# A graph network on one Trainium2 core: every other turn's eighth source tile picked column by column by ScalarE instead of gathered

## The reference

```python
hs = h[src]
m = sum_b coef[etype, b] * (hs @ bases[b])        # layers 0-2; layers 4, 5: (x @ W[etype])[src]
h_new = relu(segment_sum(m, dst, n) + h @ loopw + bias)
```

## Time and profile before

| | |
|---|---|
| Median of 3 runs | 7757.05 us (7752.96 to 7761.15) |
| The profiled execution | 7750.85 us, of which the span from the first to the last instruction is 7749.0 us |
| GpSimd busy | 5606.2 us (72%) |
| TensorE (PE) busy | 5240.5 us (68%) |
| VectorE (DVE) busy | 3236.1 us (42%) |
| ScalarE (ACT) busy | 1009.2 us (13%) |
| TensorE's granted clock, mean | 0.682 of full speed |
| Indirect gathers in relational layers | 3276 + 819 |

### The profile page before, as it was taken

How to read it: one execution, slowest core, us unless ns; L and a number is a source line. 1 busy time by engine, 2 the same in 40 slices (tenths; PEclk the granted TensorE clock), 3 DMA queues, 4 the chain that set the end, 5 groups by cost and what they waited for, 6 DMA issues and landing times. The chain is left out here.

```text
span 7749.0 us, 133241 instructions
## 1 busy us (share of the span) xinstructions
PE 5240.5 (68%) x25966; PEld 4651.5 (60%) x25967; DVE 3236.1 (42%) x10580; ACT 1009.2 (13%) x2622; POOL 5606.2 (72%) x6200
## 2 busy tenths in 40 slices
PE   6777777777776666667777777667776766544444
PEld 5667666766656555667666766556655655533333
DVE  5454454554555555544444662222223333212222
ACT  1111111111111111122222011111111111100000
POOL 6777767777767777677777337777767777677776
PEclk7777777677777777655555887777677777655555
DMA  3222222222222222222222652222222222212222
GB/s 107 79 78 76 78 75 74 78 78 78 78 55 56 57 58 57 60 66 65 66 65 66 181 148 55 57 59 57 59 54 56 58 57 59 54 53 57 55 56 54
DMA packets 348777, 538.27 MB, mean 69 GB/s; under 512 B 124457, under 2 KB 204823, under 8 KB 347975
## 3 DMA queue, kind: packets, MB, share of 16 engines
q0 software_dynamic: 184416, 378.91, 18.2%
q1 hardware_dynamic: 115315, 127.96, 5.9%
q10 hardware_dynamic: 48500, 26.51, 1.2%
HBM read 448.48 MB, written 80.14 MB: 68 GB/s over the span
## 5 line engine op out<-in xcount | busy, mean ns | idle before, releaser
L680 POOL DMA_INDIRECT ring<-h_table,edges_i x3276 | 3136.8, 958 | 1075.6 <-issue 1032.9
L968 PE MATMUL sum<-onehot,ring 128*128 128x128 f32 x8320 | 1737.9, 346 | 1014.7 <-DMA ring<-h_table,edges_i 802.0
L968 PEld LDWEIGHTS sum<-onehot,ring 128*128 128x128 f32 x8320 | 1399.2, 240 | 1313.5 <-DMA ring<-h_table,edges_i 778.5
L1267 DVE TENSOR_TENSOR acc<-msg,acc 128x16 f32 x4160 | 727.7, 175 | 2682.4 <-PE msg L975 2167.2
L975 PE MATMUL msg<-work,mix_w 128*128 128x128 f32 x4992 | 1032.3, 391 | 278.6 <-ACT work L760 271.7
L975 PEld LDWEIGHTS msg<-work,mix_w 128*128 128x128 f32 x4992 | 954.3, 294 | 352.5 <-issue 332.6
L760 ACT ACTIVATE work<-sum 128x512 f32<-128x512 f32 x1040 | 619.9, 597 | 3719.2 <-PE sum L968 3631.6
L629 POOL DMA_INDIRECT sorted_rows<-ring,pos_i x832 | 805.8, 969 | 283.0 <-issue 245.8
L680 POOL DMA_INDIRECT ring<-in_x_dram,edges_i x819 | 798.8, 975 | 280.8 <-issue 253.9
L661 POOL DMA_INDIRECT ring<-h_table,pos_i x832 | 786.7, 945 | 275.3 <-issue 275.3
L975 PE MATMUL msg<-work,rel_w 128*128 128x128 f32 x3328 | 731.8, 409 | 182.8 <-ACT work L760 181.0
(11 more groups left out here) (197 smaller groups left out, 3628.1 us busy)
## 6 DMA issues: line engine op xcount, KB each, us to landing
lent<-h_table SPq DMA_DIRECT2D x6656, 0.5 KB
ring<-sorted_rows SPq DMA_DIRECT2D x208, 260.0 KB, 3.1
ring<-h_table,edges_i POOLq DMA_INDIRECT x3276
edges_i<-bucket_flat SPq DMA_DIRECT2D x208, 208.0 KB
lent<-in_x_dram SPq DMA_DIRECT2D x1664, 0.5 KB
h_table<-rows ACTq DMA_DIRECT2D x78, 256.0 KB
ring<-h_table SPq DMA_DIRECT2D x832, 8.0 KB
sorted_rows<-ring,pos_i POOLq DMA_INDIRECT x832
```

The lines of the kernel that those rows point to most:

```text
L680: nc.gpsimd.indirect_dma_start(out=rows_in[:, s, :], out_offset=None, in_=rows_of[:, :], in_offset=bass.IndirectOffsetOnAxis(ap=srcT_i[:, ...
L968: last = nc.tensor.matmul(SUM[q % 2][:, t * KEYS:(t + 1) * KEYS], rows_in[:, 4 * q + t, :], onehot[:, 4 * q + t, :], start=True, stop=True)
L1267: nc.vector.tensor_tensor(acc[:, at], MSG[h][:, s * WIN:(s + 1) * WIN], acc[:, at], ALU.add).then_inc(added, 1)
```

## The change

In layers 0, 2, 4 and 5 (not 1) GpSimd skips tile 7 (`PICKED`) in turns 2, 4, ..., 50. In place of each skipped gather ScalarE copies the 128 source columns of the transposed table into `picks` [128 x 128], 64 in a turn, so that a tile is filled over two turns. It does 16 after each quarter's evacuation: it loads 16 source numbers into registers and issues 16 ACTIVATEs of 128x1, each with a source and a destination column that lie in registers. At the end of every turn TensorE waits for the 64 picks, transposes `picks` into `SUM[1]`, and ScalarE copies the result into slot 7 or, after a turn with only half of a tile, into a part of the ring that nothing reads. TensorE waits for that copy (`picks_placed`) before quarter 1 of the next turn. The source numbers of the next turn come by a DMA of 64 numbers, issued by ScalarE at the end of a turn. In layer 1 ScalarE only raises the four semaphores.

```diff
+PICKED = HALF - 1
+PICKS = D // 2
 # GpSimd
+                                if s == PICKED and picks_in_layer(l) and i and i % 2 == 0:
+                                    continue
 # ScalarE
+                    def list_picks(i):
+                        at = nc.s_assert_within(act.snap(i // 2 * (2 * RING * D - D) + i * PICKS + (2 * RING + PICKED) * D),
...
+                        act.dma_start(picks_i[:, :], src[bass.ds(at, PICKS)].rearrange("(o e) -> o e", o=1)).then_inc(picks_in, 16)
+                    def pick(i, k, q):
+                        each = PICKS // 4
+                        if q == 0:
+                            act.wait_ge(picks_in, k * 16 + 16)
+                            apart(act)
+                            act.wait_ge(picks_turned, k + 1)
+                            apart(act)
...
+                        _, sources = nc.values_load_multi_w_load_instructions(
+                            picks_i[0:1, q * each:(q + 1) * each], engines=[ACTIVATION], min_val=0, max_val=N_NODES - 1,
...
+                        for e in range(each):
+                            last = act.activation(picks[:, bass.ds(first + (q * each + e), 1)],
+                                                  nodes[layer["src"]][:, bass.ds(sources[e], 1)], ACT.Copy)
+                        if q == 3:
+                            last.then_inc(picks_set, 1)
+                    def place(i, k):
+                        list_picks(nc.s_assert_within(act.snap(i + 1 - (i + 13) // 64 * TURNS), min_val=0, max_val=TURNS - 1,
...
+                        act.wait_ge(picks_turned, k + 2)
+                        act.wait_ge(summed[1], k + 2)
...
+                        act.activation(ring[:, bass.ds(to, D)], SUM[1][:, 0:D], ACT.Copy).then_inc(picks_placed, 1)
 # ScalarE's evacuate, behind each quarter's copy and at the end of the turn
+                                if picks_in_layer(l):
+                                    pick(i, k, q)
+                        if picks_in_layer(l):
+                            place(i, k)
 # TensorE's messages
+                                if q == 1:
+                                    pe.wait_ge(picks_placed, k + 1)
...
+                        if picks_in_layer(l):
+                            pe.wait_ge(picks_set, k + 1)
+                            nc.tensor.transpose(SUM[1][:, 0:D], picks[:, :], ident[:, :]).then_inc(picks_turned, 1)
```

More of the change, by code:

```diff
@@ L34 @@
 SP = mybir.EngineType.SP
+ACTIVATION = mybir.EngineType.Activation
 D = 128
@@ L424, in build, with picks_in_layer, gathers, gathers_before @@
         rows_from = [x] + [tables[(l - 1) % 2] for l in range(1, len(LAYERS))]
-        def gathers(s):
+        def picks_in_layer(l):
+            return l != 1
+        def gathers(s, l):
+            if s == PICKED and picks_in_layer(l):
+                return 16 * (TURNS // 2 + 1)
             return GATHER_PASS - 16 * QUADS if s == RING - 1 else GATHER_PASS
+        def gathers_before(s, l):
+            return sum(gathers(s, n) for n in range(l) if LAYERS[n]["kind"] == REL)
         def apart(eng):
@@ L606, in _ @@
             nc.gpsimd.memset(group_end[:, 0:1], 0).then_inc(lanes_set, 1)
+            nc.gpsimd.memset(picks[:, :], 0.0).then_inc(lanes_set, 1)
             pool.wait_ge(src_in, 16)
@@ L685, in _ @@
                         pool.wait_ge(summed[3], count(P, p, r, TURNS) + 1)
+                        pool.wait_ge(picks_placed, count(P, p, r, TURNS) + 1)
                         apart(pool)
                         for h in range(2):
-                            pool.inc_swdge_sem(gathered[HALF * h:HALF * (h + 1)], [gathers(s) for s in range(HALF * h, HALF * (h + 1))],
+                            pool.inc_swdge_sem(gathered[HALF * h:HALF * (h + 1)], [gathers(s, l) for s in range(HALF * h, HALF * (h + 1))],
                                                mode="sub")
@@ L744, in _ @@
                     chunk_loop(act, lambda c, j, n: start_acc(layer, c, j))
+                    if l == 0:
+                        for n in range(4):
+                            act.wait_ge(x_in[n], 16)
+                        act.wait_ge(lanes_set, 7)
+                    elif layer["src"] == "x":
+                        act.wait_ge(x_kept, CHUNKS * NORM_BEFORE[l] + 2)
+                    else:
+                        act.wait_ge(y_kept, CHUNKS * KEPT_BEFORE[l])
                     def keep_pos(i):
@@ new lines, in pick @@
+                    def pick(i, k, q):
[5 more added lines that the diff above has]
+                            apart(act)
+                        first = nc.s_assert_within(act.snap(i * PICKS - i // 2 * D), min_val=0, max_val=PICKS,
+                                                   skip_runtime_bounds_check_because="the half of a tile by the turn's parity")
+                        _, sources = nc.values_load_multi_w_load_instructions(
+                            picks_i[0:1, q * each:(q + 1) * each], engines=[ACTIVATION], min_val=0, max_val=N_NODES - 1,
+                            skip_runtime_bounds_check_because="sources are numbers of nodes")
+                        for e in range(each):
[3 more added lines that the diff above has]
+                            last.then_inc(picks_set, 1)
@@ new lines, in place @@
+                    def place(i, k):
+                        list_picks(nc.s_assert_within(act.snap(i + 1 - (i + 13) // 64 * TURNS), min_val=0, max_val=TURNS - 1,
+                                                      skip_runtime_bounds_check_because="one of the turns, the first one behind the last"))
+                        act.wait_ge(picks_turned, k + 2)
+                        act.wait_ge(summed[1], k + 2)
+                        to = nc.s_assert_within(act.snap(i // 2 * (2 * (UNUSED - PICKED * D)) + UNUSED - i * (UNUSED - PICKED * D)),
+                                                min_val=PICKED * D, max_val=UNUSED,
+                                                skip_runtime_bounds_check_because="one of two places by the turn's parity")
+                        act.activation(ring[:, bass.ds(to, D)], SUM[1][:, 0:D], ACT.Copy).then_inc(picks_placed, 1)
@@ L954, in messages @@
                     def messages(i, k):
[L956 removed]
+                        gathers_there = pe.snap((i * 3 + 2) // QUAD * 16 + (gathers_before(RING - 1, l) + 16))
                         lent_there = pe.snap((k + 1) // QUAD * 16 + 1)
```

48 lines of the change are left out of this document (32 added, 16 removed).

## The result

The changed kernel takes 7849.33 us (median of 4 runs, 7834.92 to 7856.55) against 7755.01 for the kernel before on the same chip: 1.0119 times as long, 95% interval [1.0106, 1.0133]. It is 94 us slower where 70 us faster was forecast. The second rival came, and near its own price (7844 us), though by chance: not by the term that priced it, as will be seen.

The account below looks back on a forecast made before the run. GpSimd's gathers were taken to bound the kernel: 7750.85 us, less 76 saved in layers 2, 4 and 5, plus 6 lost in layer 0, gave 7681; with 6.2 for the median, 7687 us, range 7635 to 7850.

Parts of the forecast that it names:

- The second rival: ScalarE's batch behind quarters 0 and 2 becomes the bound: slower, 7844 us at 0.17 us a pick; chance 0.22.
- the ceiling: Layers 0, 2, 4 and 5: 25 fewer gathers each save 126.7 us, reached only where GpSimd stays slowest.
- The batch: ScalarE, one quarter's evacuation to the earliest next: load 0.95, 16 picks of 0.135, waits 0.1, so 3.2 us.
- the whole 0.6 of the forecast: Loop through ScalarE and TensorE: 0.6 us a turn for transposing and for waits ahead of the first pick.
- the backward branch: End of ScalarE's loop body: a pause of nothing to 3.0 us; taken as nothing, 3 us kept for the range.
- The loop: ScalarE and TensorE, one turn: 11.8 + 0.6 + 2 x 3.2 = 18.8 us, under GpSimd's 19.1; layer 0, 19.9.
- first step: TensorE's stretches, quarter 1 to 2 and 3 to 0: 11.8 us together, in layer 0 5.4 + 7.5 = 12.9.
- second step: TensorE's clock: if denser turns get the upper level more often, each stretch is up to 1.7 us shorter.
- break-even: Batch length at which the loop costs as much as the old turn: 3.56 us overall, a pick of 0.157.
- the last turn's batch: End of a layer: batch and placing behind the last gather, 1 us given back per layer.
- SyncE's 19.4 us a turn: Layer 0, SyncE's lending: 77.6 us for four turns, 19.4 a turn; near, not first.
- margin of 0.3 us: Layers 2, 4 and 5: 18.8 us a turn through ScalarE and TensorE against GpSimd's 19.1, 0.3 us to spare.

Follow-up runs that it names:

- the control: Kernel before the change plus twelve useless TensorE products a turn in layers 0, 2, 4 and 5: 7759.71 us against 7762.25, ratio 0.9998.

## Why the prediction was wrong

**Right.** GpSimd set the turn before (the control, and the ceiling of 122 to 124 us against 126.7). The 794 gathers, their unchanged length. The batch: picks 0.125 us apart for 0.135, a load of 1.02 for 0.95, and from quarter 2 to quarter 3 6210.51 - 6207.35 = 3.16 us for 3.2. Quarter 0 to 1 is 3.80, since the two waits there put the first pick 0.63 us later (1.21 for 0.58 us of idle before it), which is the whole 0.6 of the forecast, set down for it and the transposition together. No pause shows at the backward branch: quarter 0 waits for TensorE's sums (1.28 and 0.48 us in the rows above). The loop as the place that decides, and the second rival's mechanism.

**Wrong, first step: the length of TensorE's two stretches,** "I take 11.8 together" and, for layer 0, 5.4 + 7.5 = 12.9. They are 5.94 + 6.72 = 12.7 in layer 4 and 6.22 + 8.76 = 15.0 in layer 0. I had read them from one turn each, and those were short turns. The means of before stood in the same trace: 5.78 + 8.42 = 14.2 in layer 0, 1.3 us above my reading, and 12.2, 5.81 + 6.32 = 12.1 and 11.8 in layers 2, 4 and 5, so that there the reading is at most 0.4 us short. The rest is growth. The turn shown above takes 3.80 + 6.42 + 3.16 + 5.41 = 18.8 us, exactly the forecast, but it is a short one again: the median turn of that layer is 19.1 us and the mean 19.50, as every fourth or fifth turn, where a chunk closes, takes 20 to 22 and nothing absorbs it. With 14.2 the forecast for layer 0 would have been 14.2 + 0.6 + 6.4 = 21.2 us against 20.3, a loss of some 47 us where I wrote 6.

**Wrong, second step: the sign of the clock, in layer 0.** "If denser turns get the upper level more often" the stretches would be shorter. The batches don't make TensorE's turns denser, they cut them: it stands still 3.0 and 3.6 us ahead of each set of messages. In layer 0 the mean granted clock fell from 0.72 to 0.69, a message product takes 410 ns where it took 383, and the stretches went from 14.2 to 15.0 us. Of these 0.8 us 0.44 lie in quarter 1 to 2, where no transposition stands; how the rest, in quarter 3 to 0, divides between clock and transposition (0.27 us in the row above) wasn't measured alone.

```profile
L975 PE MATMUL msg<-work,mix_w 128*128 128x128 f32 x1664 | 334.4, 383 | 92.7 <-ACT work L760 91.0 <-DVE acc L1267 1.7
```

```profile
L1057 PE MATMUL msg<-work,rel_w 128*128 128x128 f32 x3328 | 709.2, 399 | 737.7 <-ACT work L826 737.7
```

The first line is layer 0 of before, the second layers 4 and 5 of after. In layers 4 and 5 the clock explains no growth: the products took 409 ns before and take 399, though the stands ahead of them went from 0.9 to 3.5 us. TensorE's mean granted clock was 0.73 and 0.75 there before, and is 0.74 and 0.75. They were as slow already. The stretches of layers 2, 4 and 5 grew by 0.4, 0.5 and 0.7 us all the same, of which 0.5, 0.4 and 0.4 came from quarter 3 to 0, where the transposition now stands. So the 0.6 us of the sum, used up by the waits ahead of the first pick, was too small as well; what fills the stretch besides the transposition stays open.

Twelve products (218 us back) and batches moved (217 us back) are each enough to undo the whole loss, the first by a TensorE faster than before, the second by shorter stands. The Trainium skill, "TensorE: Matmul & The Clock Gate", section "What's actually happening", says that the throttled state is the default and that activity releases it; the useless products agree (409 to 311 ns in the kernel before), and it should have stood among the rivals.

**Right time, wrong term.** The rival's 7844 us was reckoned with a batch of 3.77 us, a pick of 0.17 us. The batch was 3.2. Its price lay on all 208 turns, while the whole loss came in the 52 of layer 0; that 7844 and 7849 lie so close is chance. Its break-even didn't hold: with the mean stretches of before the loop passes the old turn of layer 0 at 2B = 20.3 - 14.2 - 0.6, a batch of 2.75 us, and not at 3.3.

**Smaller misses.** I gave 1 us for the last turn's batch behind the last gather. From the end of a layer's last gather to the first of the next it is 5732.9 - 5707.2 = 25.7 us in layer 4 (before: 16.9) and 26.8 in layer 0 (before: 15.4): the backlog of a loop that is slower than GpSimd, paid once a layer, 9 to 11 us. The end of layer 2, ScalarE and TensorE behind the last gather of 3288.54:

```profile
3287.74 0.60 ACT L826 ACTIVATE work<-sum 128x512 f32<-128x512 f32 x1 [2.31 <-PE sum L1050]
3288.54 0.95 POOL L699 DMA_INDIRECT ring<-h_table,edges_i  x1 [0.31 <-issue]
3289.38 2.10 ACT L801 ACTIVATE picks<-hT  x16 [1.04 <-issue]
...
3291.38 0.59 ACT L826 ACTIVATE work<-sum 128x512 f32<-128x512 f32 x1
3292.21 3.46 PE L1057 MATMUL msg<-work,mix_w 128*128 128x128 f32 x16 [2.88 <-ACT work L826]
```

ScalarE evacuates quarter 0 when the turn's last gather is being issued; before, it was quarter 2. SyncE's 19.4 us a turn in layer 0 was never reached: the shortest mean turn there is 19.71, with products in both halves. The ends given for a batch, 2.5 and 5.1 us, come to 2.4 and 5.2 by their own terms, which changes nothing.

The range's upper end, 7850, was drawn at a pick of 0.17 us; that it just held the result is luck. The chance of 0.22 for slower was too low: of the terms of the loop only the batch had been given a spread, though its margin of 0.3 us was no larger than what the one turn of the earlier trace rows lacks to the mean of its layer (0.3 us), and far smaller than that of the earlier trace rows (1.3 us).

## What to carry to other kernels

Where a change makes a loop through two engines nearly as long as the pace of the engine that bounds, reckon the loop from means over all turns, not from one, for what one turn is over no other makes up. Put an engine's extra work where the partner has work of its own, not between a result and the instruction that waits for it: here the same 64 copies made the kernel 94 us slower or 123 us faster, by their place alone. And where TensorE is on the path, count its stands and look at the clock behind them: products filling stands of 3.0 to 3.6 us brought 218 us here, and nothing in the kernel before, which GpSimd bounds.

## What was not expected of the hardware

- Twelve useless products a turn, on an engine whose work is on the path, take 218 us off 7849 (1.0119 to 0.9844 of the kernel before). They fill stands of 3.0 to 3.6 us, and in the turns shown the products behind them go from 3.5 and 3.8 to 2.05 and 2.19 us for sixteen records.
- A 128x1 activation with both addresses in registers starts every 0.125 us, with one register operation of 64 ns before each. The Trainium skill, "ScalarE: Activation LUTs", section "Rules for kernel authors", has one budget about 0.3 us for an activation with a pointer operand; these have none, and the measurement is far below it.
- One chip ran this kernel in 10571 us where the others took 7753 to 7762, with gathers as long as elsewhere (956 and 958 ns in the kernel without copies) and long stands between them. Ratios measured there (1.028 for a kernel that is 0.985 elsewhere) even have another sign.
